# State space mixer and tree FFN on one core: VectorE's norm statistics and the B product of state 12 placed into ScalarE's two table steps, silu placed behind the copy of the output rows

## What is computed

```python
h = _layernorm(x) * (1 + ca) + sa
x = x + ga * mamba(h)
h = _layernorm(x) * (1 + cb) + sb
x = x + gb * tree_ffn(h)
```

```python
xp, z = split(h @ W_in)
u = silu(causal_depthwise_conv(xp))
dt_r, B, C = split(u @ W_xp)
delta = softplus(dt_r @ W_dt + dt_bias)
# per token t, channel e, state n:
h_state = exp(delta * A[e, n]) * h_state + delta * u * B[n]
y = sum_n(h_state * C[n]) + u * D_skip
out = (y * silu(z)) @ W_out
```

## Time and profile before

| | us |
|---|---|
| runs of the kernel before | 494.99, 493.28, 495.41 (median 494.99) |
| the profiled execution, its own time | 494.61 |
| its span, first to last instruction | 492.8 |
| VectorE busy | 450.6 (91%) |
| GpSimd busy | 430.3 (87%) |
| TensorE busy, matmuls | 409.5 (83%) |
| ScalarE busy | 376.3 (76%) |

### The profile page before, as it was taken

The page is one execution under the profiler, slowest core; times in us unless marked ns, Lnnn a source line. Parts: engine busy times, 40 slices in busy tenths (PEclk is TensorE's granted clock), DMA queues, the critical chain, the costliest instruction groups (busy, mean ns, idle before and its releaser), DMA issues. The chain is left out here.

```text
span 492.8 us, 6755 instructions
## 1 busy us (share of the span) xinstructions
PE 409.5 (83%) x2172; PEld 278.1 (56%) x2172; DVE 450.6 (91%) x534; ACT 376.3 (76%) x689; POOL 430.3 (87%) x241
## 2 busy tenths in 40 slices
PE   7979766997599798997789798997899798688696
PEld 4436444674358456674648556664657456565374
DVE  5898899989999899989999889988999889999872
ACT  2467986598877898697977898698966897787825
POOL 4868899999999789988999899988999789999810
PEclk8989987998899989998999989998999988799999
DMA  6583036200831018300642018300642018300000
GB/s 177 151 312 138 1 107 260 87 0 1 289 121 45 1 39 330 108 0 2 234 164 77 2 41 328 107 1 0 240 161 76 0 42 326 107 2 21 0 23 21
DMA packets 23716, 51.06 MB, mean 104 GB/s; under 512 B 4474, under 2 KB 13825, under 8 KB 19585
## 3 DMA queue, kind: packets, MB, share of 16 engines
q1 hardware_dynamic: 23680, 50.64, 29.3%
HBM read 48.01 MB, written 2.62 MB: 103 GB/s over the span
## 5 line engine op out<-in xcount | busy, mean ns | idle before, releaser
L609 POOL TENSOR_TENSOR hc<-h,c_rows 128x1024 f32<-128x1024 f32 x127 | 298.3, 2367 | 26.8 <-DVE h L1368 26.7
L1368 DVE TENSOR_TENSOR_SCAN h<-dA,state,dbu 128x512 f32<-128x512 f32 x192 | 234.3, 1266 | 13.2 <-ACT dA L697 13.2
L697 ACT ACTIVATE dA<-delta,a_neg 128x512 f32<-128x512 f32 x256 | 173.2, 685 | 46.7 <-DVE h L1368 46.2
L1121 PEld LDWEIGHTS yb<-ident,hc 128*128 128x128 f32 x1024 | 130.0, 148 | 63.4 <-issue 43.7
L1121 PE MATMUL yb<-ident,hc 128*128 128x128 f32 x1024 | 154.0, 286 | 7.4 <-POOL hc L609 7.4
L1381 DVE TENSOR_TENSOR dbu<-du,bb 128x1024 f32<-128x1024 f32 x88 | 105.5, 1199 | 4.1 <-PE bb L1147 3.8
L596 POOL TENSOR_TENSOR dbu<-du,b_rows 128x1024 f32<-128x1024 f32 x40 | 94.6, 2366 | 3.9 <-DMA b_rows<-bc_dram 3.9
L1368 DVE TENSOR_TENSOR_SCAN h<-dA,dbu 128x512 f32<-128x512 f32 x64 | 74.2, 1206 | 5.5 <-ACT dA L697 5.4
L1147 PE MATMUL bb<-b_parts,sel 128*128 128x512 bf16 x88 | 35.1, 399 | 43.1 <-DVE dbu L1381 41.7
L1021 PE MATMUL mf<-f_hT,w_conv 128*128 128x512 f32 x112 | 55.1, 617 | 2.0 <-ACT zu L757 1.4
L1147 PEld LDWEIGHTS bb<-b_parts,sel 128*128 128x128 bf16 x88 | 8.7, 99 | 56.1 <-DVE dbu L1381 35.5
(11 more groups left out here) (206 smaller groups left out, 534.2 us busy)
## 6 DMA issues: line engine op xcount, KB each, us to landing
c_rows<-bc_dram SPq DMA_DIRECT2D x32, 1024.0 KB, 8.0
b_rows<-bc_dram SPq DMA_DIRECT2D x40, 256.0 KB, 9.4
xs<-in_L_attn_x_dram SPq DMA_DIRECT2D x8, 256.0 KB, 4.0
out_dram<-xs SPq DMA_DIRECT2D x7, 256.0 KB, 5.5
ygT<-in_L_attn_conv_w_dram SPq DMA_DIRECT2D x1, 512.0 KB, 5.7
bc_dram<-xd SPq DMA_DIRECT2D x8, 64.0 KB, 1.6
probT<-in_L_wmod_dram SPq DMA_DIRECT2D x1, 384.0 KB, 4.6
w_in<-in_L_attn_W_in_dram SPq DMA_DIRECT2D x1, 256.0 KB, 4.4
```

The costliest lines, as they stand in the source:

```text
L609: nc.gpsimd.tensor_tensor(hc[:, pair % RC, :, :], h[:, pair % RH, :, :], c_rows[:, q, n % NQ, :].unsqueeze(1).broadcast_to([P, HALVES, T]) ...
L697: nc.scalar.activation(dA[ke % RD][:, :], delta[:, ge % 2, half, :], ACT.Exp, scale=a_neg[:, half, n:n + 1]).then_inc(s_dA, 1)
L1121: last = nc.tensor.matmul(bank[:, tile], hc[:, pair % RC, half, tile], ident[:, :], start=False, stop=n == N - 1 if last_of_bank is None e ...
L1368: v.tensor_tensor_scan(h[:, pair % RH, half, :], dA[k % RD][:, :], dbu[:, pair % RW, half, :], start, ALU.mult, ALU.add).then_inc(s_scan, 1)
```

## The change

The change only moves instructions:

- ScalarE's silu step goes from step 10 to step 11 (`F_SILU`), and in the code the copy of the output rows is put ahead of the silu block. So at step 11 there come dA 13, the copy of the output rows and then the table load. The copy of the tree's result at step 25 (`ff`, the same lines) goes ahead of that step's last copy to `b_parts` with it.
- The `dt` products on TensorE go one step on, to 12, 13 and 14, 15, since they read silu's result.
- The second norm's statistics go from behind scan 14 to behind scan 13 (`T_STATS`).
- `dbu` of state 12 is made at step 19 and no longer at step 22, behind scan 19 and, in groups 0 to 3, behind the first norm's statistics (which the diff puts ahead of the `dbu` for this). The fill of its bank goes to the head of TensorE's step 19 (from step 21). A new function `made_at` says at which step a pair's `dbu` and fill stand.

```diff
@@ -77,14 +77,15 @@
     AHEAD_EXP, AHEAD_FILL, AHEAD_DBU, LAG_SUM = 2, 3, 2, 5
+    N_EARLY, K_EARLY = 12, 19
...
-    F_SILU, F_SP, F_DU = 10, 17, (25, 26)
+    F_SILU, F_SP, F_DU = 11, 17, (25, 26)
...
-    T_GATE, T_STATS, T_RSTD, T_OFF, T_XHAT = (4, 5), 14, 19, 20, 24
+    T_GATE, T_STATS, T_RSTD, T_OFF, T_XHAT = (4, 5), 13, 19, 20, 24
@@ -93,8 +94,8 @@
-              ("dt", 0): (1, (11, 12)), ("xd", 0): (1, (18, 19)), ("tr", 0): (2, (28,))},
+              ("dt", 0): (1, (12, 13)), ("xd", 0): (1, (18, 19)), ("tr", 0): (2, (28,))},
-        "t": {("yt", 0): (-1, (6,)), ("yt", 1): (-1, (8,)), ("out", 0): (-1, (10,)), ("dt", 1): (1, (13, 14)),
+        "t": {("yt", 0): (-1, (6,)), ("yt", 1): (-1, (8,)), ("out", 0): (-1, (10,)), ("dt", 1): (1, (14, 15)),
@@ -382,6 +383,15 @@
+        def made_at(k, ahead):
+
+            g, n = divmod((k + ahead) // HALVES, N)
+            if k >= 0 and k % STEPS == K_EARLY:
+                return k // STEPS * N + N_EARLY
+            if (k + ahead) % HALVES == 0 and 0 <= k + ahead < K and n not in POOL_N and n != N_EARLY:
+                return g * N + n
+            return None
@@ -756,6 +766,12 @@
+                    for name in ("out", "ff"):
+                        for g2 in due(name, 0, g, s):
+                            wait_job(act, "t", name, 0, g2)
+                            nc.scalar.activation(xs[:, g2 * TILES:(g2 + 1) * TILES, :],
...
                     if g >= 0 and s == F_SILU:
@@ -1131,9 +1141,9 @@
-                    kf, ks = k + AHEAD_FILL, k - LAG_SUM
-                    if 0 <= kf < K and kf % HALVES == 0 and kf // HALVES % N not in POOL_N:
-                        pair = kf // HALVES
+                    ks = k - LAG_SUM
+                    pair = made_at(k, AHEAD_FILL)
+                    if pair is not None:
@@ -1367,9 +1377,10 @@
-                    kd = k + AHEAD_DBU
-                    if 0 <= kd < K and kd % HALVES == 0 and kd // HALVES % N not in POOL_N:
-                        pair = kd // HALVES
+                    if 4 <= g + 4 < GROUPS and s == N_STATS:
+                        stats(g + 4, f_bn, f_mv[:, g + 4, :, :], s_fvar)
+                    pair = made_at(k, AHEAD_DBU)
+                    if pair is not None:
@@ -1381,8 +1392,6 @@
-                    if 4 <= g + 4 < GROUPS and s == N_STATS:
-                        stats(g + 4, f_bn, f_mv[:, g + 4, :, :], s_fvar)
```

More of the change, by code:

```diff
@@ L758, in _ @@
                                                  ACT.Copy).then_inc(s_read["f"], 1)
+                    for name in ("out", "ff"):
+                        for g2 in due(name, 0, g, s):
+                            wait_job(act, "t", name, 0, g2)
+                            nc.scalar.activation(xs[:, g2 * TILES:(g2 + 1) * TILES, :],
+                                                 job("t", name, 0, g2)[1][:, :].rearrange("p (i d) -> p i d", d=DM),
+                                                 ACT.Copy).then_inc(s_read["t"], 1)
                     if g >= 0 and s == F_SILU:
@@ L814, in _ @@
                             nc.scalar.activation(ygT[:, half, :], job("t", "yt", half, t)[1][:, :],
-                                                 ACT.Copy).then_inc(s_read["t"], 1)
-                    for name in ("out", "ff"):
-                        for g2 in due(name, 0, g, s):
-                            wait_job(act, "t", name, 0, g2)
-                            nc.scalar.activation(xs[:, g2 * TILES:(g2 + 1) * TILES, :],
-                                                 job("t", name, 0, g2)[1][:, :].rearrange("p (i d) -> p i d", d=DM),
                                                  ACT.Copy).then_inc(s_read["t"], 1)
```

## The result

| | before | after |
|---|---|---|
| median of the runs beside each other, us | 494.13 (4 runs) | 499.88 (4 runs, 498.62 to 500.42) |
| profiled execution, its own time / span | 494.61 / 492.8 | 500.42 / 498.6 |

The ratio is 1.0107 with a 95% interval of 1.0085 to 1.0129: the changed kernel is slower, by 5.7 us beside the runs of before of that comparison and by 4.9 beside the 494.99 of the first table. The prediction said 3.3 us.

The account below looks back on a forecast made before the run. VectorE (91% busy) looked like the bound, with holes; ScalarE bounds the softplus stretch to dA 28. Silu steps +3.7, dt products 0, softplus -0.4: 494.99 + 3.3 = 498.3 us, range 494.3 to 500.5.

Parts of the forecast that it names:

- its own forecast: Whole kernel: 498.3 us, 3.3 us more than before, within 497.2 to 499.5; chance 0.63.
- the two terms: Silu steps +3.7 us (slower) and softplus steps -0.4 us (faster).
- Silu step, +3.7: Table load waits for `out`, starting 2.97 us later; 0.62 to 0.74 us lost in groups 1 to 6, 0.3 gained in group 0.
- dt products, 0: TensorE held some 1.9 us for silu of u; products and fill of state 9 still in time, cost 0.
- the 0.7 us of the rival: Half clock on the `dt` products delays the fill of state 9 by 0.7 us in each of six groups.
- Softplus step, -0.4: Early `dbu` fills the hole ahead of scan 20, but ScalarE bounds to dA 28; 0.4 us gained, bounds 0 to 3.9.
- Group 7, 0.1: Last group's silu step, only silu of z left and no hole on VectorE: 0.1 us lost.
- The sum: Profiled execution 494.61 + 3.7 - 0.4 = 497.9 us; from the median, 494.99 + 3.3 = 498.3 us.
- The rival with TensorE at half clock: Half clock on the `dt` products delays the fill of state 9: +4.2 us, giving 502.5; chance 0.08.
- Holes in the busiest engine: Both VectorE holes, silu and softplus steps, filled with no later `dA`: 11.1 us gained, giving 483.9; chance 0.07.

Follow-up runs that it names:

- the silu part alone: The change with `dbu` of state 12 back at step 22, against the kernel before: 503.33 us, ratio 1.016.
- the second profile: Profile of the changed kernel run again unaltered, against the kernel before: median 499.57 us, ratio 1.0114.

## Why the prediction came out as it did

It said 498.3 with a range of 494.3 to 500.5, and 497.2 to 499.5 for its own forecast; 499.88 and 499.57 were measured. The direction was right, and so was the place of the main loss, the silu step. The size was 1.6 us short: 3.3 us more than before instead of 5.7. The measured time lies inside the wide range and outside the narrow one, and the upper end of the wide range was not set for what happened. One of the two terms had the wrong sign.

- **Silu step, +3.7.** Right, by the numbers and by the cause: 2.98 for the 2.97 us between the two starts of the load, 0.62 us lost in groups 1, 5 and 6, 0.69 and 0.74 in groups 4 and 3. With the 0.36 us that group 0 gains, the silu part alone loses 4.13 - 0.36 = 3.8 us in these steps by its trace. Group 2 loses 0.73 or 0.74 where I took group 5's value; it differs from the others by 0.1. That the load waits for `out` was tested: without that wait and its copy in front, the same kernel is 6.9 us faster.
- **dt products, 0.** Right as to VectorE: the fill has 2.00 us in hand. It held at 1.2 GHz too. TensorE waits 2.06 us ahead of the first `dt` product in each of the groups 1 to 6, and the stretch at 0.50 fell on these products in the groups 2, 4 and 6 in the first profile of the change and in 1, 3 and 5 in the second. View by windows, group 6 of the first:

```profile
389.70:393.10 3.40, 3.40 (x9) 1.64 (x8) 1.26 (x4) 3.37 (x6) 1.40 (x1) 0.50 0.00 0
```

  Group 6 loses 0.62 us in its silu step in both profiles and nothing behind it, so the 0.7 us of the rival did not come.
- **Softplus step, -0.4: the step that failed.** The part on ScalarE's chain held within 0.03 us (scan 28 of group 5 gains nothing, group 3 gains 0.26 of the 0.27). What failed is the sentence that groups 0 and 1 "have no hole" and so cost 0. A `dbu` put where there is no hole delays the scans behind it by 0.8 to 1.1 us until the place that it came from is reached, and I asked only whether VectorE gets this back. In groups 0 to 3 GpSimd, at 87% busy, waits for those very scans; in group 3 the rows show that it has no idle time behind. By the trace of its own run the early `dbu` costs 1.4 + 0.4 - 0.3 = +1.5 us instead of -0.4, a difference of 1.9 where 1.6 were missing.
- **Group 7, 0.1.** Near at 2.4 GHz (0.11 at scan 15 and another 0.11 behind it in the second profile), some 1.6 us short in an execution at 1.2 GHz.
- **The sum** was made against a profiled execution that had lost 1.5 us at its start to the clock, and stood near the median all the same. There is one trace only of the kernel before, so what its other executions lose to the clock, and where, is not known.
- **The rival with TensorE at half clock** named a loss that exists, at the wrong place. I priced it at the `dt` products, where there is slack. It costs time where ScalarE copies TensorE's result inside a full chain, at the path sums: 1.3 to 2.0 us for a stretch there. In seven such losses (four of them behind scan 23 of group 2 or 5, one of group 6, two at scan 16 of group 7) a wait of TensorE of 1.9 us or more stood ahead, as in the earlier trace rows. Others came behind shorter waits: the 1.34 us in group 7 of the run with `dbu` early in 4 to 6 only behind one of 1.09, those behind the last scan behind waits of 0.9 to 2.0. That the same wait can also be followed by 2.4 GHz is what group 7 of the change showed.
- **Holes in the busiest engine.** That rival would have given 483.9. Filling holes gave 1.0011 in groups 4 to 6 and a loss in the rest. The advice of the Trainium skill (Perfetto Trace Analysis, Identifying the Most-Contended Engine) to optimize the busiest engine first does not say where the gain is here. The moves that gained were made in the list of ScalarE, at 76%: dA 13 ahead of the silu step with the waiting copy left behind it, and `ff` behind dA 28, which gained once VectorE's hole was filled too.

## To carry to other kernels

Before putting work into an engine's hole, look at what stands on the other side of it: if the engine that ends the hole is itself busy to the next meeting point, the time comes back as a wait there. Here only a move on both engines gained. Where the same table of steps serves groups with and without the hole, cost the move in those without it on every engine that the delayed instructions release, and not only on the engine whose list is changed. And a wait moved ahead of a serial block (here two table loads) is paid by all that stands behind the block: the same silu step, one step later, loses 0.6 to 0.75 us a group behind the copy that waits, and gains 0.4 to 0.6 ahead of it.

## What the runs showed of the hardware

The stretches of 1.2 GHz fall on other places from one execution of the same kernel to the next: the changed kernel waited 2.50 and 2.51 us on TensorE and got 0.50 and 1.00 as the clock behind it. The Trainium skill (TensorE: Matmul & The Clock Gate, part 1) says that the activity window runs freely, and that the number of matmuls at half rate at the start of a kernel therefore varies from run to run. These profiles show such a variation in mid-kernel too. One such stretch costs nothing where TensorE has slack (the `dt` products of group 6) and 1.3 to 2.0 us where ScalarE waits for the product. It is as large as what an edit like this moves, so the groups' differences between two profiles have to be cleared of it before they are read as an effect.

A table switch costs its load and no more here, with work on both sides of it: in the changed kernel the copy ends at 330.31, the load at 330.33 takes 1.28 us and silu starts at 331.62. The Trainium skill (ScalarE: Activation LUTs, What ACT_TABLE_LOAD costs) adds a drain of about 1.38 us to each switch; the rows here have no room for it on either side of the load, and the measurement decides.
